# A fused recurrence phase on one core: small products packed into parts of the TensorE array, and a new order of the work

## The reference, cut to what matters

```python
shifted = jnp.pad(h, ((0, 0), (1, 0), (0, 0)))[:, :T_]
delta = shifted - h
x_lerp = h + delta * x_proj_mu
x0 = jnp.tanh(x_lerp @ xl_w1.T) @ xl_w2.T + xl_b2
x1 = jnp.tanh(x0).reshape(B_, T_, 5, R)                       # R = 32
x2 = jnp.einsum('btnr,hnr->btnh', x1, x_out_w.reshape(H_, 5, R))
mus = x2 + x_bias
r_mu, w_mu, k_mu, v_mu, g_mu = (mus[:, :, i] for i in range(5))
r = (h + delta * r_mu) @ r_w.T
w = jnp.tanh((h + delta * w_mu) @ w_w1.T) @ w_w2.T + w_b
k = (h + delta * k_mu) @ k_w.T
v = (h + delta * v_mu) @ v_w.T
g = (h + delta * g_mu) @ g_w.T
wd = jnp.exp(-jnp.exp(w.reshape(B_, T_, NH, DK)))
def step(S, xs):
    r_t, k_t, v_t, w_t = xs
    o_t = jnp.einsum('bhk,bhkv->bhv', r_t, S) + jnp.sum(r_t * bonus * k_t, -1, keepdims=True) * v_t
    S = S * w_t[..., None] + k_t[..., None] * v_t[..., None, :]
    return (S, o_t)
```

## Time and profile before

| | |
|---|---|
| median of 3 runs | 4390.36 us (4386.61 to 4394.35) |
| profiled execution, its own time | 4401.49 us |
| profiled execution, span | 4399.7 us |
| TensorE busy | 4125.3 us (94%) |
| VectorE busy | 2703.7 us (61%) |
| ScalarE busy | 1936.3 us (44%) |
| GpSimd busy | 1696.7 us (39%) |
| the recurrence | about 187 to 1765 us of the span |

### The profile page before, as it was taken

How to read it: one execution, slowest core, us unless ns; L and a number is a source line. 1 busy time by engine, 2 the same in 40 slices (tenths; PEclk the granted TensorE clock), 3 DMA queues, 4 the chain that set the end, 5 groups by cost and what they waited for, 6 DMA issues and landing times. The chain is left out here.

```text
span 4399.7 us, 72682 instructions
## 1 busy us (share of the span) xinstructions
PE 4125.3 (94%) x28636; PEld 3270.7 (74%) x28636; DVE 2703.7 (61%) x5040; ACT 1936.3 (44%) x3576; POOL 1696.7 (39%) x1337
## 2 busy tenths in 40 slices
PE   8699999999999998899999999999995999999995
PEld 8656656656656655798898988888895888888884
DVE  7467777777777776344434343444432688888885
ACT  2134444444444444445444444545442444444441
POOL 2234334334334332444434444444433234444443
PEclk9999999999999998999999999999997999999998
DMA  9501011011011010333323232332224344454433
GB/s 313 168 25 35 30 39 35 30 40 35 30 40 35 30 40 20 92 49 59 62 42 65 47 61 43 66 51 57 43 40 98 98 102 110 100 116 112 106 68 43
DMA packets 254003, 294.21 MB, mean 67 GB/s; under 512 B 21600, under 2 KB 226656, under 8 KB 251616
## 3 DMA queue, kind: packets, MB, share of 16 engines
q0 software_dynamic: 88064, 117.74, 15.8%
q1 hardware_dynamic: 165600, 171.82, 12.1%
HBM read 155.15 MB, written 134.35 MB: 66 GB/s over the span
## 5 line engine op out<-in xcount | busy, mean ns | idle before, releaser
L564 DVE TENSOR_TENSOR e_hTl<-e_hf,e_hTh 128x512 fp32r<-128x512 f32 x512 | 354.6, 692 | 800.5 <-ACT e_hTh L506 752.2
L1077 POOL TENSOR_TENSOR a_mix<-a_tmp,a_h 128x512 f32<-128x512 f32 x320 | 389.9, 1238 | 793.8 <-PE ps L1376 745.1
L425 POOL DMA_INDIRECT acc_d<-e_y,e_sids x256 | 409.0, 1598 | 707.4 <-DVE e_y L580 654.6
L505 ACT ACTIVATE e_hf<-ps_heads,e_b 128x512 f32<-128x512 f32 x512 | 355.4, 694 | 677.3 <-PE ps_heads L663 620.8
L663 PE MATMUL ps<-e_w2h,e_hTh 128*128 128x256 f32 x2048 | 578.8, 283 | 0.0
L663 PE MATMUL ps<-e_w2h,e_hTl 128*128 128x256 f32 x2048 | 577.3, 282 | 0.0
L663 PE MATMUL ps<-e_w2l,e_hTh 128*128 128x256 f32 x2048 | 571.3, 279 | 1.0 <-issue 1.0
L663 PE MATMUL ps_heads<-e_xTh,e_w1h 128*128 128x512 f32 x1024 | 418.4, 409 | 16.2 <-ACT e_hTh L506 8.8
L663 PE MATMUL ps_heads<-e_xTh,e_w1l 128*128 128x512 f32 x1024 | 405.5, 396 | 0.0
L663 PE MATMUL ps_heads<-e_xTl,e_w1h 128*128 128x512 f32 x1024 | 405.4, 396 | 0.0
L663 PEld LDWEIGHTS ps<-e_w2h,e_hTh 128*128 128x128 f32 x2048 | 385.7, 188 | 20.4
(11 more groups left out here) (293 smaller groups left out, 9218.0 us busy)
## 6 DMA issues: line engine op xcount, KB each, us to landing
r_x<-in_L_attn_hidden_states SPq DMA_DIRECT2D x32, 512.0 KB, 6.2
xn_d<-r_xn SPq DMA_DIRECT2D x32, 512.0 KB, 4.8
xnT_d<-r_xT SPq DMA_DIRECT2D x32, 512.0 KB, 3.8
acc_d<-a_zeros POOLq DMA_DIRECT2D x32, 512.0 KB, 3.0
s_d<-a_s SPq DMA_DIRECT2D x32, 512.0 KB, 2.8
e_w<-in_L_ffn_w SPq DMA_DIRECT2D x16, 1024.0 KB
f_a<-acc_d SPq DMA_DIRECT2D x32, 512.0 KB, 3.8
f_x<-s_d SPq DMA_DIRECT2D x32, 512.0 KB, 5.2
```

What stands on the lines that cost most here:

```text
L425: pool.indirect_dma_start(acc_d, bass.IndirectOffsetOnAxis(ap=sids[:, GT * q + t:GT * q + t + 1], axis=0), ys[r][:, t, :], None, compute_o ...
L505: nc.scalar.activation(hf[m % 2][:], ps[2 + m % 2][:], ACT.Gelu, bias=b1s[:, m:m + 1])
L564: nc.vector.tensor_tensor(hT[q % 2][1][:, m, :], hf[m % 2][:], hT[q % 2][0][:, m, :].bitcast(F32), ALU.subtract).then_inc(h_sb, 1)
L1077: nc.gpsimd.tensor_tensor(mix[n][:, m, :].rearrange("p (c t) -> p c t", c=GT), tmp[i % 2][:].rearrange("p (c t) -> p c t", c=GT), h[q % 2] ...
```

## The change

Four things change, all in the recurrence.

1. Packing. LOW runs as four products of 128 columns in four column parts of the array (128 rows by 32 columns each), for four sequences, so that `low` is one 128x128 tile. X0 becomes four products with weights padded into the rows of each sequence, X0T eight in column parts. The first eight MIX products run in pairs, one in rows 0 to 63 and one in rows 64 to 127 of the array, each into a bank of its own; the last two are four half products in the same row parts. DLOW runs in two column parts, DEXP as two products of half the width.
2. Banks. `BANKS` gives each result a bank by hand: DLOW, KEY, two MIX, REC and OWN go to the score banks 0 to 3 after the last level.
3. Diagonals. ScalarE writes the diagonals of two heads (8 instructions instead of 16), GpSimd those of the other two in one instruction of 1024 elements a partition; level 0's selection waits for both.
4. Order. `sequence` is written out anew: the interpolations behind the selections of levels 0 and 1, all three instructions of the top-value round behind level 6, VAL and GATES behind levels 0, 1 and 2, OWN and the diagonals right before level 0. GpSimd makes the diagonals before the last two mixes.

```diff
+        PIECES, LATE = 15, 12
+        LOW, X0, X0T, DLOW, KEY, DEXP, REC, OWN, VAL, GATES = 0, 1, 2, 9, 10, 13, 14, 17, 18, 20
+        MIX = [3, 4, 5, 6, 7, 8, 11, 12, 15, 16]
+        MIXED = [(1, 0), (2, 0), (1, 1), (2, 1), (0, 0), (3, 0), (0, 1), (3, 1), (4, 0), (4, 1)]
+        BANKS = [6, 7, 6, 7, 6, 7, 6, 7, 6, 0, 1, 2, 3, 7, 0, 7, 6, 1, 6, 7, 6, 7]
+        AT = {2: (0, 1), 3: (2, 3), 4: (4, 5), 7: (6, 7), 10: (8, 9)}
+        BY_POOL = 2
         def bank(n):
-            return ps[6 + n % 2]
+            return ps[BANKS[n]]
...
+            for g in range(GROUPS):
+                level(g, 0)
+                piece(g, 12)
+                if g + 1 < GROUPS:
+                    begin(g + 1, 0)
+                level(g, 1)
+                preceding(g - 1, 2)
+                if g + 1 < GROUPS:
+                    begin(g + 1, 1)
+                piece(g, 13)
+                level(g, 2)
+                preceding(g - 1, 3)
+                piece(g, 14)
+                following(g + 1, 0)
+                level(g, 3)
+                preceding(g - 1, 4)
+                following(g + 1, 1)
+                level(g, 4)
+                following(g + 1, 2)
+                preceding(g - 1, 5)
+                level(g, 5)
+                preceding(g - 1, 6)
+                following(g + 1, 3)
+                level(g, 6)
+                preceding(g - 1, 7)
+                following(g + 1, 4, 5)
+                step(g, 5)
+                step(g, 6)
+                preceding(g - 1, 8)
+                following(g + 1, 6, 7)
+                step(g, 7)
+                chunk(g, 0)
+                if g + 2 < GROUPS:
+                    ahead(g + 2)
+                following(g + 1, 8, 9, 10, 11)
+                chunk(g, 1)
...
+            def diagonal(f):
+                r, hs = f % 2, slice(NH - BY_POOL, NH)
+                emptied(pool, f, OWN)
...
+                nc.gpsimd.tensor_tensor(A2[r][:, hs], ident[:].unsqueeze(1).unsqueeze(1).to_broadcast(shape),
+                                        own[:, :, hs].rearrange("p c h -> p h c").unsqueeze(3).to_broadcast(shape), ALU.mult
+                                        ).then_inc(diag_rest, 1)
+
+            def piece(f, s):
+                if s == 10:
+                    return
+                if s == 11:
+                    diagonal(f)
+                    s = 10
...
                 if lv < LEVELS - 2:
                     if lv == 0:
                         dve.wait_ge(diag_sb, g + 1)
+                        dve.wait_ge(diag_rest, g + 1)
...
-                    for hd in range(NH):
+                    for hd in range(NH - BY_POOL):
                         for c in range(GT):
                             done = nc.scalar.activation(A2[r][:, hd, c, :], ident[:], ACT.Copy, scale=own[:, c, hd:hd + 1])
...
+                def side_by_side(i):
+
+                    to = [room(MIX[i]), room(MIX[i + 1])]
+                    rows = [slice(0, P // 2), slice(P // 2, P)]
...
+                    for v in range(2):
+                        n, m = MIXED[i + v]
+                        nc.tensor.matmul(to[v][:], xo[rows[v], n, m * P:(m + 1) * P], x1[rows[v], :], start=True, stop=True
+                                         ).then_inc(piece_ps, 1)
...
                 if s == 0:
+                    to = room(LOW)
                     pe.wait_ge(lerped, 2 * f + 2)
-                    product(room(LOW)[0:RANK, :], [(w1[:, k, :], lerp[:, k, :]) for k in range(KD)]).then_inc(piece_ps, 1)
+                    for k in range(KD):
+                        for c in range(GT):
+                            done = nc.tensor.matmul(to[RANK * c:RANK * (c + 1), 0:P], w1[:, k, :],
+                                                    lerp[:, k, c * P:(c + 1) * P], start=k == 0, stop=k == KD - 1)
+                    done.then_inc(piece_ps, 1)
```

More of the change, by code:

```diff
@@ L868, in recurrence_phase @@
         NMM = NMU * KD
-        LOADS = 21
-        PADDED = 7
+        PADDED = 4
+        LOADS = 14 + GT + 2 + GT + GT + NMU - 1
         SET = PADDED + 8
         READY = SET + NH + 2
[L873 to L881, removed]
+        PIECES, LATE = 15, 12
+        UNITS = 9
+        LOW, X0, X0T, DLOW, KEY, DEXP, REC, OWN, VAL, GATES = 0, 1, 2, 9, 10, 13, 14, 17, 18, 20
+        MIX = [3, 4, 5, 6, 7, 8, 11, 12, 15, 16]
+        MIXED = [(1, 0), (2, 0), (1, 1), (2, 1), (0, 0), (3, 0), (0, 1), (3, 1), (4, 0), (4, 1)]
+        BANKS = [6, 7, 6, 7, 6, 7, 6, 7, 6, 0, 1, 2, 3, 7, 0, 7, 6, 1, 6, 7, 6, 7]
+        USES = len(BANKS)
+        BY_ACT = [LOW, X0, X0T, DLOW, KEY, DEXP, REC, OWN, VAL, VAL + 1]
         BY_DVE = MIX + [GATES, GATES + 1]
-        AT = {2: (0, 1), 3: (2, 3), 4: (4, 5), 6: (6, 7), 7: (8, 9)}
+        AT = {2: (0, 1), 3: (2, 3), 4: (4, 5), 7: (6, 7), 10: (8, 9)}
+        BY_POOL = 2
         def pairs_ps(half):
@@ L946, in sequence, with following @@
[L946 to L960, removed]
+            def following(f, *pieces):
+                if f < GROUPS:
+                    for s in pieces:
+                        piece(f, s)
@@ L962, in recurrence_phase @@
+            for u in range(2, UNITS):
+                chunk(GROUPS - 1, u)
         block = mem.enter_context(nc.Block())
@@ L993, in store @@
[L993 to L1019, removed]
+                    to, first = h[q % 2][:, k], P * j - 1
+                    if j == 0:
+                        to, first = h[q % 2][:, k, :, 1:P + 1], 0
@@ new lines, in last_mix @@
+                def last_mix(i):
+                    to = [room(MIX[i]), room(MIX[i + 1])]
+                    emptied(pe, f, X0T)
+                    for u in range(2):
+                        for v in range(2):
+                            rows = slice(P // 2 * v, P // 2 * (v + 1))
+                            done = nc.tensor.matmul(to[v][:, HALF * u:HALF * (u + 1)], xot[rows, u, v * P:(v + 1) * P],
+                                                    x1t[rows, :], start=True, stop=True)
+                            if u:
+                                done.then_inc(piece_ps, 1)
@@ L1459, in level @@
                 else:
-                    emptied(pe, g, REC)
-                if not first or lv:
+                    emptied(pe, g, OWN)
+                    emptied(pe, g, MIX[7])
+                if n:
                     pe.wait_ge(A_sb, n)
```

388 lines of the change are left out of this document (193 added, 195 removed).

## The result

The changed kernel takes 4450.94 us (median of 4, 4446.66 to 4456.44) against 4388.48 for the kernel before in the same runs: a ratio of 1.0149, 95% interval 1.0137 to 1.0162. It is slower by 62 us, outside the range, on the side that the forecast had at 0.21.

What follows compares the result with a forecast made beforehand. TensorE was taken to bound the recurrence; six steps summed to 45.95 us a group against 47.22, saving 39 us in 31 periods, plus 5 at the start: 44 us, so 4390 becomes 4346. Range 4265 to 4425.

Steps and rivals of the forecast that it cites:

- The port lock: VectorE with two SBUF inputs and GpSimd mixes wait for each other; level 0 to 1 takes 7.4 us instead of 4.99.
- the diagonal: GpSimd's instruction of 1024 elements a partition right before level 0, taken as 1.89 us like `delta`.
- The overlap of packed products: Paired MIX products run fully at once: four pairs save 3.4 us, all packing 6.6 us of TensorE a group.
- The first group: Its wait for `delta` before level 0 goes: 5 us saved with shorter products at the start, between 0 and 8.
- rival B: Idle time before level 1 drops TensorE's clock to 1.2 GHz; at 5 us low, period 48.45 and 4423 us; chance 0.28.
- the new pause: TensorE's idle time before level 1, 2.9 us, taken as shorter than both pauses after which the clock had fallen.
- step 1 to 2: From level 1 to level 2 in a group, with o and GATES on TensorE: 5.5 us against 4.70 before.
- The break-even: The change gains nothing if low clock adds 1.4 us a group, when about 2.8 us pass at the low level.
- Rival C: Packed products don't overlap; three pairs and DLOW behind level 6 cost 3.4 us more: period 49.3, 4451 us; chance 0.06.
- The top-value rounds: Behind level 6, they lie in VectorE's spare time of some 5 us; otherwise their 4 us would be on the path.
- step 6 to 0: From level 6 to the next level 0: 17.4 us plus 0.6 for changes of array parts, 18.0 against 18.56 before.
- The ten more loads: On SP, each under half a microsecond, hidden under VectorE's setup; without that cover they would cost 4 us.

Runs made afterwards that it cites:

- fill1: Changed kernel with the second half of VAL computed twice, 1.75 us more TensorE work between level 0 and level 1; 4322.19 us, ratio 0.987 to the kernel before.
- diag_act: Changed kernel with all sixteen diagonals on ScalarE, none on GpSimd; 4454.32 us, ratio 1.0172 to the kernel before.
- mix_wait_diag: Changed kernel with GpSimd waiting for level 0's decays before mixes 8 and 9, and all sixteen diagonals on ScalarE; 4454.73 us, ratio 1.0172.
- unpacked: Changed kernel with the first eight MIX products over all 128 rows again, one after the other; 4474.66 us, ratio 1.022 to the kernel before.
- before_pause: Kernel before, with level 1 on TensorE also waiting for ScalarE's copy of the state of the group before; 4489.45 us, ratio 1.0193.
- old_order: Changed kernel's packing, banks and split diagonals, but with the sequence put back to the order of the kernel before; 4365.44 us, ratio 0.9968.
- mix_wait: Changed kernel with one added wait: GpSimd waits for level 0's decays before mixes 8 and 9; 4261.74 us, ratio 0.9734 to the kernel before.
- fill_half: Changed kernel with only the last quarter of VAL computed twice, 0.87 us more TensorE work before level 1; 4399.43 us, ratio 0.9992.

## Why the prediction was wrong

**Right: where the time goes without the clock.** Every step but one came within 0.35 us: 7.14 for 7.4, 3.6 for 3.45, 7.44 for 7.75, 3.51 for 3.85, 18.20 for 18.0. The port lock behaves as the rows of before said, one instruction of each engine in turn, and the diagonal was as long as `delta`. The Trainium skill's rule (SBUF — State Buffer, Who interferes with whom) held beside the mixes and the diagonal: R took 1.41 us with a mix in front of it and 0.41 without. It did not hold beside GpSimd's power, in the changed kernel as in the one before: K took 0.42 us at 742.43 while rstd ran from 742.00 to 744.93. The overlap of packed products was right; a pair took 1.06 us where 0.87 and a share of the changes of parts had been taken, so it saves 0.66 us and not 0.86. In the argument for it, the 0.98 us of the earlier trace rows are those of a level's weight loads; its 32 products took 1.12, which is still well under the 1.7 of no overlap.

**Right, with a gap: the ends.** The first group took 45.15 us from its level 0 to the next, 5.2 less than before (50.37); its first level 0 started 0.6 us earlier, for 5 us taken. The last group and the end of the recurrence, 10.8 us longer, had no term in the sum. In fill1, without low stretches in the groups, they were 5.3 longer.

**Wrong: the clock.** The step that failed is 1 to 2, put at 5.5 us, where 9.46 were measured, since the forecast had the clock stay up and gave rival B 0.28. The argument against a fall was that the new pause "is shorter than both of those, which speaks against a fall". That premise was false. TensorE's timeline of the kernel before has the two pauses behind which the clock fell in the earlier trace rows:

```profile
246.93 1.62 PE L1467 MATMUL ps_heads<-a_R,a_K 32*128 32x64 f32 x32 [4.41 <-DVE a_A L1203]
...
1718.69 1.99 PE L1467 MATMUL ps_heads<-a_R,a_K 32*128 32x64 f32 x32 [2.47 <-DVE a_A L1203]
```

The second is 2.47 us, shorter than the 2.9 that were forecast, and the level behind it took 1.99 us instead of 1.12. So the trace of before spoke for a fall, and from this row B should have had the larger chance. The runs bear it out. Of the 30 steady groups the clock fell in 29 with a pause of 2.4 us (30 with the 2.5 of diag_act and mix_wait_diag, 23 in unpacked), in 19 with the 2.3 of before_pause and the 1.9 of old_order, in 16 with 1.5, and in none where no pause was over 0.9 (mix_wait, fill1). Pauses of nearly one length give 19 to 29, so the length isn't all that decides; what else does is open. Without the falls, 3.82 us a group less, the changed kernel would be 4451 - 118 = 4333; fill1, where this was done, has 0.987 of the kernel before, or 4331 of 4388. The forecast was 4346.

**Wrong in rival B too: its size.** It was sized at up to 5 us of low clock a group, and 4423; the changed kernel has 8.3 us a group. The low stretches of before last 3.4 and 10.2 us in its trace, the second still low at 1728 in the earlier trace rows, and I took a value between them. That half of each low us is lost was about right: 0.47 in step 1 to 2 of the changed kernel (3.82 us for 8.1 in a steady group). The break-even came out above the 2.8 us of the forecast, since the steps saved more than 1.4 us a group: fill_half passes 3.7 us a group at the low level (116 over 31) and takes as long as the kernel before. The range's upper end of 4425 fell with the size.

**Right for no reason.** Rival C, products that don't overlap, gave 4451, the time that was measured. Its mechanism is not there.

**The top-value rounds** moved behind level 6 seem to lie beside other work, as costed: step 6 to 0 is 18.20 for 18.0; no run moved them alone. The ten more loads cost nothing that shows: level 0 of the first group starts at 237.1 us, and at 237.7 before.

## What to carry to other kernels

When a change frees an engine, lay out the new order step by step and look for the longest single pause of TensorE; a pause of 2.4 us made the step that it lies in 2.2 us longer here, and the next 3.8 us more through the clock. Look for the shortest pause in the trace of before behind which the clock fell; here one row, 2.47 us in the last group, spoke against the forecast. Where VectorE and GpSimd both read two operands from SBUF (GpSimd's power was an exception here), keep GpSimd's queue from starting next to the short VectorE instructions on the path, and let it run beside those with one operand in SBUF; a single wait did that here and was worth 182 us. Through the clock, a step on the path can even be shortened by work added in the pause before it.

## What the runs showed of the hardware

The added products of fill1 made the kernel 122 us faster; the granted clock was 1.00 in all its steady groups, and 0.62 and 0.52 in step 1 to 2 of the two groups shown without them. A pause of 2.30 us in the kernel before gave low stretches of 3.4 us in 19 of 30 groups, one of 2.40 us in the changed kernel gave 6.8 or 10.2 us in 28, 3.4 in one and none in one. K took 0.43 and 0.42 us beside GpSimd's power, which has two operands in SBUF, and 1.42 behind the start of a mix. A selection (one operand in SBUF, one in PSUM) ran in 2.45 us beside two mixes and in 2.41 alone.
